# Two Mamba and mixture-of-experts layers on one core: layer 0's shared output added to X from PSUM, rows zeroed at the start, four gathers ahead, 23 tiles, layer 1's routed experts three slots later

## Chip, cores and metric

One core of a Trainium2 chip. The metric is the device time of one execution in microseconds (us), the median of several; lower is better.

## The reference

Four sublayers add to the residual stream `x` (2048 rows of 512, fp32). Twice: a selective scan over a context, gated by the normalised `x`, and then a mixture of experts of the new `x`.

```python
x = x + L0_xattn(ctx, layernorm(x))     # u = silu(conv(in_proj ctx)); state = state*exp(d*A) + d*u*B_t
                                        # y = sum_n state*C_t + D*u;  y * silu(z), z = layernorm(x)
x = x + L0_ffn(layernorm(x))
#   logits = x @ router_w; e = argmax; score = sigmoid(max)
#   out  = silu(xs @ gate_w[e]) * (xs @ up_w[e]) @ down_w[e],  xs = x * score
#   out += silu(x @ shared_gate_w) * (x @ shared_up_w) @ shared_down_w
x = x + L1_xattn(ctx, layernorm(x))     # the same form, other weights
x = x + L1_ffn(layernorm(x))            # softmax, top 2 of 8 experts of width 352,
                                        # shared expert of width 1408 times a sigmoid gate
```

Scan: 4 batches, 512 channels, 512 steps, 16 states. Experts: 8.

## The kernel before

The 2048 rows are T = 16 tiles of 128 rows, held in SBUF as `X`. All is fp32. Every engine's order is written out by hand; semaphores join the engines. Four stages stand one after the other, with the semaphores cleared between them.

**Projections** (`stage_proj`, to about 136 us) make `u` of both layers; those of layer 1, and B and C of both, go to DRAM.

**Scans** (`scan_stage`, 136 to 1434 us). 32 groups (2 layers x 4 batches x 4 channel tiles) of 16 states, 512 slots in all. A slot is `exp` on ACT into a PSUM bank (L528), `dBu` on POOL (L561), the scan on DVE (L608), the product with C on DVE (L592), and the sum over states by a matmul with the identity (L474). ACT may be at most three slots ahead of DVE's L592, POOL one ahead of L608. Four groups are a batch of 64 slots, `vb` 0 to 7; (vb, n) names a slot.

`Beside` puts layer 0's experts beside the scans, as pieces after each slot. In slots 15 to 63 of vb = 1 to 3 and 15 to 50 of vb = 4, `Shared` does one batch's four tiles: five turns r of 14 pieces m, so that down products of a tile run in the turn after its gate. It normalises into `xn` (L933), transposes, and multiplies by gate, up and down (L957). `copy_y` on ACT (L1023) takes the down product out of PSUM bank 7 into `yo`, and SP stores it in `sh_d` (L1051). `yo` is the same buffer as `sg`, so the tanh of the next tile (L1038) waits until that store has landed. `xn` is also the scratch for the tanh of the gate z (L879). At the end of vb = 4 the rows are routed; in vb = 5, `scatter` normalises and scales each tile on ACT from `X` (L1248) and POOL scatters it by expert into `xs_d` (L1256). `xs_d` was zeroed by one large DMA each (`zeros`, L424) at slot 20 of vb = 0 and 1. From slot 25 of vb = 5, `Experts` runs two pieces a slot: 24 tiles of 128 routed rows, with one buffer each for gate, up and down weights. A tile's down product again comes one turn later and its store two turns later; what is left over when the slots end runs after them.

**Layer 1's feed-forward** (`stage_ffn1`, 1434 to 2346 us). `front(b, p)` prepares batch b: add `sh_d` (L1468) and the gathered routed output of layer 0 (POOL L1416, DVE L1472) to `X`, statistics (L1475, L1478), z, silu, transposes (L1580), the new `X`, the second norm, `xTb` and the router logits (L1593). front(0) runs alone; fronts 1 to 3 run beside slots 0 to 14 of the 60 `SLOTS`, 8 sub-steps each. A slot is one 128-wide chunk of the shared expert (8 matmuls, L1612) or one tile's down product (11 matmuls, L1626). SP issues, in order: two loads of `sh_d`, the router's weights, the two halves of gate and up (2.8 MB each), the down weights (2.8 MB), and only then the next two loads of `sh_d`. Routing stands in slots 15 to 18; then POOL scatters 16 tiles to two experts each (L1453). From slot `FIRST` = 21, `Experts(1)` puts one turn of 14 pieces beside each slot: 39 tiles, of which two turns are left after the last slot.

**Combine** (`stage_combine`, 2346 to 2402 us) gathers the two rows of each token and adds them.

## Time and profile before

| | us |
|---|---|
| median of 3 runs | 2396.59 (2393.40 to 2399.49) |
| profiled execution, its own time | 2404.08 |
| span of its trace | 2402.1 |

| engine | busy us | share |
|---|---|---|
| PE (matmul) | 1959.0 | 82% |
| DVE | 1415.0 | 59% |
| POOL | 989.3 | 41% |
| ACT | 855.9 | 36% |

DMA moved 352.5 MB, 147 GB/s over the span. No engine is busy all through: the shares are means over stages with different limits. A PE record is half of an fp32 matmul here: a 128x512 product shows as two records, 0.43 us from start to start at 2.4 GHz.

### The profile page before, as it was taken

To read this page: it belongs to the slowest core of one execution; us is meant where nothing else is said; L and a number is where in the kernel's file an instruction comes from. 1 tells how busy PE (TensorE), PEld (TensorE's weight loads), DVE (VectorE), ACT (ScalarE), POOL (GpSimd) and SP (SyncE) were. 2 spreads that over 40 slices of the span, in tenths; PEclk is the share of its full clock that TensorE was granted. 3 is DMA by queue.
4 is the path that set the end of the run, shared out by engine and by line. 5 is a ranking of instruction groups with operands and counts; after the bars stand their busy time and mean duration, and the time that the engine had idled before them with its cause. 6 is when DMAs were issued, how large, how long until landed. Compare 5 with 4: busy or idle time off the path is not lost. (4 is left out here: it accounts for less than half of the span.)

```text
span 2402.1 us, 18775 instructions
## 1 busy us (share of the span) xinstructions
PE 1959.0 (82%) x5107; PEld 901.3 (38%) x5107; DVE 1415.0 (59%) x1962; ACT 855.9 (36%) x1392; POOL 989.3 (41%) x889
## 2 busy tenths in 40 slices
PE   8837678788787795599999973889599999999990
PEld 2212233233233341144444432445255555555540
DVE  6869988888887878797888844654010111111113
ACT  5545545364544444555656420110011111111110
POOL 0057766666575665887777731211400000000005
PEclk9968889899898997799999985999799999999995
DMA  5044354302203004368687645211654555455536
GB/s 185 22 194 105 140 110 107 112 5 99 89 8 153 1 14 155 138 225 339 224 305 277 215 153 189 68 50 58 242 179 152 180 180 166 160 179 180 175 123 214
DMA packets 100992, 352.50 MB, mean 147 GB/s; under 512 B 15200, under 2 KB 15200, under 8 KB 82464
## 3 DMA queue, kind: packets, MB, share of 16 engines
q1 hardware_dynamic: 93216, 326.21, 39.7%
q0 software_dynamic: 7680, 25.17, 3.1%
q8 instruction: 41, 0.67, 0.1%
q14 instruction: 55, 0.45, 0.1%
HBM read 288.29 MB, written 63.05 MB: 146 GB/s over the span
## 5 line engine op out<-in xcount | busy, mean ns | idle before, releaser
L561 POOL TENSOR_TENSOR work<-work,big 128x512 f32<-128x512 f32 x512 | 658.5, 1291 | 265.7 <-DVE bank L608 263.9
L474 PE MATMUL bank<-work,ident 128*128 128x512 f32 x928 | 536.9, 693 | 226.5 <-DVE work L592 175.9
L608 DVE TENSOR_TENSOR_SCAN bank<-bank,work 128x512 f32<-128x512 f32 x512 | 624.9, 1221 | 137.5 <-ACT bank L528 88.9
L528 ACT ACTIVATE bank<-work,An 128x512 f32<-128x512 f32 x512 | 345.9, 691 | 256.2 <-DVE work L592 253.1
L474 PEld LDWEIGHTS bank<-work,ident 128*128 128x128 f32 x928 | 179.5, 216 | 521.6 <-DVE work L592 333.7
L592 DVE TENSOR_TENSOR work<-bank,big 128x512 f32<-128x512 f32 x512 | 343.9, 672 | 9.1 <-PE bank L474 8.8
L1655 POOL DMA_INDIRECT W<-ys_d,slot x32 | 33.9, 1059 | 644.4 <-PEq L1642 634.9
L1612 PE MATMUL bank<-Y,big 128*128 128x512 f32 x528 | 263.6, 596 | 0.0
L1195 DVE SCALAR_TENSOR_TENSOR work<-work,bank 128x352 f32<-128x352 f32 (+1 forms) x63 | 36.6, 581 | 329.0 <-ACT work L1185 328.9
L957 PE MATMUL bank<-W,work 128*128 128x512 f32 x384 | 198.6, 622 | 0.0
L1173 ACT COPY work<-bank 128x512 f32<-128x512 f32 x63 | 36.9, 585 | 396.9 <-PE bank L1158 396.9
L1626 PE MATMUL bank<-big,W 128*128 128x512 f32 x352 | 169.7, 597 | 0.0
L1612 PEld LDWEIGHTS bank<-Y,big 128*128 128x128 f32 x528 | 98.8, 191 | 77.1 <-issue 48.8
L1158 PE MATMUL bank<-work 128*128 128x512 f32 (+1 forms) x234 | 115.8, 605 | 4.7 <-DMA work<-down_last 4.7
L1147 PE MATMUL bank<-work 128*128 128x352 f32 x312 | 111.5, 460 | 0.0
L1200 DVE SCALAR_TENSOR_TENSOR work<-work,bank 128x352 f32<-128x352 f32 (+1 forms) x63 | 36.6, 580 | 122.4 <-PE bank L1147 122.2
L957 PEld LDWEIGHTS bank<-W,work 128*128 128x128 f32 x384 | 75.2, 200 | 87.9 <-issue 87.9
L1137 PE MATMUL bank<-work 128*128 128x352 f32 x312 | 106.6, 465 | 1.1 <-DMA work<-gate 1.1
L1563 ACT ACTIVATE work<-bank 128x512 f32<-128x512 f32 x44 | 26.2, 596 | 220.1 <-PE bank L1612 220.1
L1158 PE MATMUL bank<-W,work 128*128 128x512 f32 x192 | 90.1, 608 | 5.6 <-DMA W<-down 5.4
L1147 PE MATMUL bank<-W,work 128*128 128x512 f32 x192 | 89.5, 604 | 0.0
L1137 PE MATMUL bank<-W,work 128*128 128x512 f32 x192 | 88.8, 593 | 0.7 <-ACT work L1166 0.7
(249 smaller groups left out, 2252.8 us busy)
## 6 DMA issues: line engine op xcount, KB each, us to landing
big<-bc_d SPq DMA_DIRECT2D x64, 1024.0 KB, 6.7
work<-gate SPq DMA_DIRECT2D x39, 704.0 KB, 4.2
work<-up SPq DMA_DIRECT2D x39, 704.0 KB, 4.1
W<-gate SPq DMA_DIRECT2D x24, 1024.0 KB, 4.9
W<-up SPq DMA_DIRECT2D x24, 1024.0 KB, 5.5
W<-down SPq DMA_DIRECT2D x24, 1024.0 KB, 5.4
work<-down SPq DMA_DIRECT2D x39, 512.0 KB, 3.8
work<-xs_d SPq DMA_DIRECT2D x63, 256.0 KB, 4.4
```

The costliest lines, as they stand in the source:

```text
L474: nc.tensor.matmul(YS[:, :], ident[:, :], hC[ring(g * NS + u[0])], start=v == 0, stop=v == len(units[g]) - 1).then_inc(sum_done, 1)
L528: nc.scalar.activation(H[i % 4][:, :], delta[g % 2], ACT.Exp, scale=An[vb // B][:, g % NJ, i:i + 1]).then_inc(dA_done, 1)
L561: nc.gpsimd.tensor_tensor(dBu[i % 2], du[g % 2], Bb[:, i, :], ALU.mult).then_inc(dBu_done, 1)
L592: nc.vector.tensor_tensor(hC[ring(s)], H[i % 4][:, :], Cb[:, i, :], ALU.mult).then_inc(hC_done, 1)
L608: nc.vector.tensor_tensor_scan(H[i % 4][:, :], H[i % 4][:, :], dBu[i % 2], 0.0, ALU.mult, ALU.add).then_inc(scan_done, 1)
L957: ins = nc.tensor.matmul(dst[:, :], at[:, c * P:(c + 1) * P], w[:, c, :], start=c == 0, stop=c == DK - 1)
L1137: ins = nc.tensor.matmul(self.G[:, 0:self.F], self.xT[q][:, c * P:(c + 1) * P], self.wg[:, c, :], start=c == 0, stop=c == DK - 1)
L1147: ins = nc.tensor.matmul(self.U[:, 0:self.F], self.xT[q][:, c * P:(c + 1) * P], self.wu[:, c, :], start=c == 0, stop=c == DK - 1)
L1158: ins = nc.tensor.matmul(self.TB[:, :], self.hT[0:fn, c * P:(c + 1) * P], self.wd[0:fn, c, :], start=c == 0, stop=c == len(self.chunks) - 1)
L1173: nc.scalar.copy(self.yo, self.TB[:, :]).then_inc(S["yo_done"], 1)
L1612: ins = nc.tensor.matmul(dst[:, :], sgu[:, c, u // DK * FS + f * P:u // DK * FS + (f + 1) * P], xTb[b][:, c, :], start=c == 0, stop=c == D ...
L1626: ins = nc.tensor.matmul(down_bank(b, r)[:, :], hT[c][:, r * P:(r + 1) * P], sdw[:, c, :], start=c == 0, stop=c == NF - 1)
```

## The change

- `Moe.tiles` is no longer made even: 23 tiles instead of 24 in layer 0.
- `copy_y`, `yo`, `sh_d`, its 16 stores and 16 loads and the 16 adds in `front` go. In `Shared.vector` DVE adds bank 7 to `X` straight away, at pieces (2,3), (3,3), (4,1) and (4,7). PE waits for `added` where it waited for `yo_done`.
- `X` then holds the shared output before the rows are scattered, so the normalised `xn` of each tile is stored in `xn_d` (SP, piece (r,6)), loaded back in vb = 5 into the scatter's row buffers, and scaled there on ACT. `norm` and the tanh into `xn` now wait for the store. 16 small copies on POOL and two small operations on DVE go.
- Both `zeros` stand in slots 0 and 1 of vb = 0, behind layer 0's weights.
- In `stage_ffn1` four gathers are under way, on four buffers; gate and up come in three pairs of loads, the first 2 chunks wide.
- `FIRST` 21 becomes 24.

```diff
-        self.tiles += (self.tiles % 2, 0)[k]
...
-                    if vb < 2 and n == 20:
-                        sp.wait_ge(hC_done, g * NS + i)
-                        zeros(vb)
+                    if g == 0 and i < 2:
+                        zeros(i)
...
             def gate(self, name, eng, b, j, i):
...
-                        self.past(eng, "xtr_done", b * NJ - NJ + (j + 1 if j else 0))
+                        used = b * NJ - NJ + (j + 1 if j else 0)
+                        self.past(eng, "xtr_done", used)
+                        self.past(eng, "xn_out", used * 16)
...
             def vector(self, dve, b, t0, n, at):
...
+                    done = {(2, 3): 0, (3, 3): 1, (NJ, 1): NJ - 2, (NJ, 7): NJ - 1}.get((r, m))
+                    if done is not None:
+                        past(dve, "d_done", t0 + done + 1)
+                        nc.vector.tensor_tensor(X[:, t0 + done, :], X[:, t0 + done, :], self.TB[:, :], ALU.add).then_inc(S["added"], 1)
...
             def norm(self, dve, b, t0, r):
...
+                self.past(dve, "xn_out", (t0 + r) * 16)
...
             def scalar(self, act, b, t0, n, at):
...
-                def copy_y(r):
-                    past(act, "d_done", t0 + r + 1)
-                    past(act, "htr_done", t0 + min(r + 2, NJ))
-                    nc.scalar.copy(self.yo, self.TB[:, :]).then_inc(S["yo_done"], 1)
-
...
-                        act.wait_ge(S["y_out"], (t0 + max(r - 1, 0)) * 16 + 1)
                         nc.scalar.activation(self.sg, self.G[:, :], ACT.Tanh, scale=0.5).then_inc(S["s_done"], 1)
...
             def sync(self, sp, b, t0, n, at):
-                for r, m in at:
-                    for tile in ([r - 2] if m == 5 and 2 <= r else []) + ([NJ - 1] if r == NJ and m == 7 else []):
-                        self.past(sp, "yo_done", t0 + tile + 1)
-                        sp.dma_start(sh_d[t0 + tile], self.yo).then_inc(self.S["y_out"], 16)
+                for tile in ([0] if n == self.START - 1 else []) + [r + 1 for r, m in at if m == 6 and r < NJ - 1]:
+                    self.past(sp, "xn_done", t0 + tile + 1)
+                    sp.dma_start(xn_d[t0 + tile], self.xn).then_inc(self.S["xn_out"], 16)
...
             def scatter(self, name, eng, t):
-                if name == "act" and 0 <= t < T:
+                if name == "sp" and 0 <= t < T:
                     if t == 0:
+                        self.past(eng, "xn_out", 16 * T)
                         eng.wait_ge(self.routed, 1)
                     if t >= 8:
                         eng.wait_ge(self.out_done[t % 8], 16)
-                    nc.scalar.activation(self.rows[t % 8], X[:, t, :], ACT.Identity, bias=nbz[:, t, 0:1],
-                                         scale=rstdx[:, t, 0:1]).then_inc(self.row_done, 1)
+                    eng.dma_start(self.rows[t % 8], xn_d[t]).then_inc(self.row_in[t % 8], 16)
+                if name == "act" and 0 <= t - 1 < T:
...
+                    nc.scalar.activation(self.rows[t % 8], self.rows[t % 8], ACT.Copy,
+                                         scale=wgt[:, 0, t:t + 1]).then_inc(self.row_done, 1)
...
-            PER_FRONT, ROUTE, FIRST = 5, 15, 21
+            PER_FRONT, ROUTE, FIRST = 5, 15, 24
+            WIDE = ((0, 2), (2, 6), (6, NF))
...
-                        at_least(pool, C["x_done"], t - 1)
+                        at_least(pool, C["x_done"], t - 3)
...
-                        if b == 0 and p < 2:
+                        if b == 0 and p < NJ:
                             gather(p)
-                        if p in (2, 3):
-                            gather(t0 + p)
-                        if b < B - 1 and p in (8, 9):
+                        if b < B - 1 and 8 <= p < 8 + NJ:
                             gather(t0 + NJ + p - 8)
...
-                            if p == r:
-                                dve.wait_ge(sh_in[t % 2], (t // 2 + 1) * 16)
-                                V.tensor_tensor(X_t, X_t, sh_b[t % 2], ALU.add).then_inc(C["sum_done"], 1)
```

On ACT, at the end of a batch of scans (the same place in vb = 1, 2 and 3). `bank<-work,An` is the exp of a slot, `COPY work<-bank` at L1023 is `copy_y`, at L1033 (L1028 in the change) the copy of the transposed h. Before:

```order
L879 ACTIVATE work<-work 128x512
L528 ACTIVATE bank<-work,An 128x512 x3
L1023 COPY work<-bank 128x512
L528 ACTIVATE bank<-work,An 128x512
L1033 COPY work<-bank 128x512
L528 ACTIVATE bank<-work,An 128x512 x3
L1023 COPY work<-bank 128x512
L528 ACTIVATE bank<-work,An 128x512 x3
```

The change:

```order
L877 ACTIVATE work<-work 128x512
L525 ACTIVATE bank<-work,An 128x512 x4
L1028 COPY work<-bank 128x512
L525 ACTIVATE bank<-work,An 128x512 x6
L868 ACTIVATE big<-X,nbz,rstdx 128x512
```

The two copies of the down product have left ACT; two and three exps that stood behind them now stand in one run with those ahead.

On SP, at the start of layer 1's feed-forward. Before:

```order
L1365 DMA work<-sh_d 128x512 x2
L1374 DMA rw<-router 128x4x9
L1378 DMA big<-sgu 128x4x1408 x2
L1379 DMA big<-sdown 128x11x512
L1365 DMA work<-sh_d 128x512 x2
```

The change:

```order
L1364 DMA rw<-router 128x4x9
L1369 DMA big<-sgu 128x4x256 x2
L1369 DMA big<-sgu 128x4x512 x2
L1369 DMA big<-sgu 128x4x640 x2
L1370 DMA big<-sdown 128x11x512
L1362 DMA xn_d<-work 128x512 x16
```

The loads on which `front` waited, two of them behind the weights, are gone.

On PE, between the router's matmuls (`bank<-work`) and the first routed tile of layer 1 (`bank<-ident,work` is its transpose). Before:

```order
L713 MATMUL bank<-work 128x128
L1612 MATMUL bank<-Y,big 128x512 x39
L1122 MATMUL bank<-ident,work 128x128 x4
L1612 MATMUL bank<-Y,big 128x512
L1137 MATMUL bank<-work 128x352 x2
```

The change:

```order
L712 MATMUL bank<-work 128x128
L1593 MATMUL bank<-Y,big 128x512 x63
L1110 MATMUL bank<-ident,work 128x128 x4
L1593 MATMUL bank<-Y,big 128x512
L1125 MATMUL bank<-work 128x352 x2
```

24 shared matmuls, three slots of 8, have come ahead of the first transpose.

## Rows read from the trace of the kernel before

**Rows 1.** Busy time by stretch: us from:to, length, each engine (xrecords), PEclk, DMA share, GB/s

```profile
285.00:950.00 665.00, 519.53 (x1250) 224.30 (x1250) 555.66 (x725) 323.73 (x490) 414.16 (x369) 0.89 0.23 76
950.00:1411.00 461.00, 412.02 (x1050) 184.97 (x1051) 385.68 (x450) 253.90 (x397) 358.12 (x286) 0.94 0.66 240
1434.00:1497.00 63.00, 15.67 (x65) 13.32 (x66) 22.59 (x45) 4.74 (x9) 10.47 (x17) 0.50 0.55 201
1497.00:1697.00 200.00, 185.48 (x558) 92.81 (x556) 109.05 (x250) 24.89 (x45) 41.77 (x65) 0.95 0.24 78
1721.00:2346.00 625.00, 619.20 (x1825) 323.25 (x1824) 84.31 (x144) 94.08 (x221) 0.00 (x0) 0.99 0.50 167
```

**Rows 2.** Waits of DVE, 285 to 950 us: for whom, us in total, times, longest

```profile
DVE bank L608 <- ACT bank L528: 40.5, 20, 5.8
...
DVE work L919 <- ACT work L1038: 21.1, 3, 7.2
```

**Rows 3.** Waits of ACT in the same stretch

```profile
ACT work L1023 <- PE bank L953: 53.4, 9, 9.1
...
ACT work L1023 <- PE bank L957: 26.3, 3, 9.0
...
ACT L1038 <- DMA sh_d<-work: 13.3, 3, 4.6
```

**Rows 4.** Timeline, end of vb = 1: start, us, engine, line, [idle before <-releaser]

```profile
440.60 0.58 ACT L1023 COPY work<-bank 128x512 f32<-128x512 f32 x1 [8.64 <-PE bank L957]
...
441.81 1.23 DVE L608 TENSOR_TENSOR_SCAN bank<-bank,work 128x512 f32<-128x512 f32 x1 [5.43 <-ACT bank L528]
```

**Rows 5.** DVE adds from PSUM (L897; ns min/median/max) and from SBUF (L1472; us, mean ns)

```profile
L897 DVE TENSOR_TENSOR X<-X,bank x16: 661/674/689, 298.4 to 800.1; 128x512 f32<-128x512 f32 x16
...
L1472 DVE TENSOR_TENSOR X<-X,work 128x512 f32<-128x512 f32 x16 | 10.9, 681 | 8.7 <-DMA work<-ys_d,slot 8.7
```

**Rows 6.** DMA issues: KB each, median us to landing

```profile
xs_d<-xds SPq DMA_DIRECT2D x1, 9984.0 KB, 52.5
```

**Rows 7.** Timeline: loads of B and C of vb = 2 asked for

```profile
255.52 0.34 SPq L419 DMA_DIRECT2D big<-bc_d  x1
```

**Rows 8.** Timeline, end of the scans and the tail behind them

```profile
1411.20 1.27 DVE L592 TENSOR_TENSOR work<-bank,big 128x512 f32<-128x512 f32 x2
...
1423.86 6.13 PE L1158 MATMUL bank<-W,work 128*128 128x512 f32 x8 [5.24 <-DMA W<-down]
```

**Rows 9.** Timeline, front(0) of layer 1's feed-forward

```profile
1434.79 1.02 POOL L1416 DMA_INDIRECT work<-ys_d,slot  x1 [24.66 <-POOLq L119]
1436.11 0.95 POOL L1416 DMA_INDIRECT work<-ys_d,slot  x1 [0.31 <-issue]
...
1464.48 0.69 DVE L1468 TENSOR_TENSOR X<-X,work 128x512 f32<-128x512 f32 x1 [19.24 <-DMA work<-sh_d]
...
1467.62 0.67 DVE L1472 TENSOR_TENSOR X<-X,work 128x512 f32<-128x512 f32 x1
```

**Rows 10.** Landing of the gathers (L1416)

```profile
DMA to landing us min/median/max: 3.3/3.7/8.3
```

**Rows 11.** Waits of PE, 1434 to 2345 us

```profile
PE bank L1580 <- DVE work L1487: 62.2, 4, 47.8
```

**Rows 12.** Timeline around slot FIRST: a run of shared matmuls, the first routed tile

```profile
1663.29 27.20 PE L1612 MATMUL bank<-Y,big 128*128 128x512 f32 x63
...
1720.72 1.11 PE L1122 MATMUL bank<-ident,work 128*128 128x128 f32 x4 [23.79 <-DMA work<-xs_d]
...
1724.64 2.69 PE L1137 MATMUL bank<-work 128*128 128x352 f32 x4 [1.10 <-DMA work<-gate]
```

**Rows 13.** Timeline: the same instruction one slot apart, and PE behind the last slot

```profile
2242.55 0.60 ACT L1563 ACTIVATE work<-bank 128x512 f32<-128x512 f32 x1 [4.41 <-PE bank L1612]
...
2257.49 0.60 ACT L1563 ACTIVATE work<-bank 128x512 f32<-128x512 f32 x1 [4.41 <-PE bank L1612]
...
2340.95 5.46 PE L1158 MATMUL bank<-work 128*128 128x512 f32 x6 [4.70 <-DMA work<-down_last]
```

More of the change, by code:

```diff
@@ L177, in program @@
         bc_d = dram("bc_d", [2 * B, 32, L])
-        sh_d = dram("sh_d", [T, P, D])
         xn_d = dram("xn_d", [T, P, D])
@@ L531, in scalar @@
                         prep(g + 1, i - y_at[g] - 3)
+                    if vb <= B:
+                        side.gate("act", act, vb, *divmod(n, NS))
                     side.step("act", act, vb, n)
@@ L820, in __init__ @@
                 self.w = w
-                made_by = {"dve": "zg_done x_done st_done mv_done xn_done h1_done h_done lg_read",
-                           "act": "z_done zt_done xT_done s_done hT_done yo_done",
+                made_by = {"dve": "zg_done x_done st_done mv_done xn_done h1_done h_done lg_read added",
+                           "act": "z_done zt_done xT_done s_done hT_done",
                            "pe": "vtr_done xtr_done g_done u_done lg_done htr_done d_done",
-                           "pool": "v_done ve_done rstd_done", "sp": "y_out"}
+                           "pool": "v_done ve_done rstd_done", "sp": "xn_out"}
                 self.made_by = {e: v.split() for e, v in made_by.items()}
@@ L853, in step @@
                 last = isinstance(b, int) and b == B
-                if not last or n < NS:
+                if name != "act":
                     self.gate(name, eng, b, *divmod(n, NS))
@@ L863, in gate @@
             def gate(self, name, eng, b, j, i):
-                first = isinstance(b, int) and b == 0
-                if first and j == 0:
+                first = b == 0
+                if first and j == 0 or b == B and j:
                     return
@@ L964, in tensor @@
                 for r, (dst, free, count) in enumerate(((self.G, "lg_read", 0), (self.U, "hT_done", 0),
-                                                        (self.TB, "yo_done", 0), (self.G, "x_done", 1))):
+                                                        (self.TB, "added", 0), (self.G, "x_done", 1))):
                     if n == self.ROUND[r]:
@@ L1001, in tensor @@
                         if r > 1:
-                            past(pe, "yo_done", t0 + r - 1)
+                            past(pe, "added", t0 + r - 1)
                         self.transpose(self.TB, self.xn, "xtr_done")
@@ L1008, in tensor @@
                             past(pe, "xT_done", t0 + min(r + 2, NJ))
-                            past(pe, "yo_done", t0 + r - 1)
+                            past(pe, "added", t0 + r - 1)
                         self.product(self.TB, self.hT, self.W0[2], m - d0, "d_done")
@@ L1027, in scalar @@
                 for r, m in at:
-                    if m == 3 and 2 <= r < NJ:
-                        copy_y(r - 2)
                     if (m == 5 if r < NJ else m == 2) and r:
@@ L1218, in __init__ @@
                 self.row_done, self.out_done = sem("t0_row_done"), [sem(f"t0_scattered{q}") for q in range(8)]
+                self.row_in = [sem(f"t0_row_in{q}") for q in range(8)]
                 self.routed, self.cleared = sem("t0_routed"), sem("t0_rows_cleared")
@@ L1234, in route @@
                         self.past(eng, "lg_read", T)
-                        self.past(eng, "rstd_done", T)
                         self.past(eng, "v_done", B * NJ)
@@ L1276, in step @@
                         eng.wait_ge(self.routed, 1)
-                        self.past(eng, "y_out", 16 * T)
+                        self.past(eng, "added", T)
+                        self.past(eng, "xn_out", 16 * T)
                     self.ex.before(name, eng)
@@ L1318, in stage_ffn1 @@
             v, zth = [wk(8 + j) for j in range(NJ)], [wk(12 + j) for j in range(NJ)]
-            sh_b, ys_b = [wk(16), wk(17)], [wk(18), wk(19)]
+            ys_b = [wk(16 + q) for q in range(4)]
             rows = [wk(14 + i) for i in range(6)]
@@ L1346, in walk @@
                             front(1 + s // PER_FRONT, s % PER_FRONT * SUB_ + u)
-                        if ROUTE <= s < FIRST:
+                        if ROUTE <= s < ROUTE + 6:
                             route(s - ROUTE, u)
@@ L1362, in _ @@
                 def _(sp):
-                    def load(t):
-                        at_least(sp, C["sum_done"], t - 1)
-                        sp.dma_start(sh_b[t % 2], sh_d[t]).then_inc(sh_in[t % 2], 16)
                     def keep(t):
@@ L1369, in keep @@
                         sp.dma_start(xn_d[t], xn[t % 2]).then_inc(xn_out[t % 2], 16)
-                    for t in range(NJ):
-                        load(t)
-                        if t == 1:
-                            sp.dma_start(rw[:, 0:DK * NL].rearrange("p (c e) -> p c e", c=DK),
-                                         w["router"].rearrange("(c p) e -> p c e", p=P)).then_inc(r_in, 16)
-                            src = w["shared_gate_up"].rearrange("(c p) f -> p c f", p=P)
-                            for c, (lo, hi) in enumerate(((0, FS), (FS, 2 * FS))):
-                                sp.dma_start(sgu[:, :, lo:hi], src[:, :, lo:hi]).then_inc(w_in[c], 16)
-                            sp.dma_start(sdw, w["shared_down"].rearrange("(c p) n -> p c n", p=P)).then_inc(w_in[2], 16)
-                    for b in range(B):
-                        for r in range(NJ):
-                            keep(b * NJ + r)
-                            if b < B - 1:
-                                load((b + 1) * NJ + r)
+                    sp.dma_start(rw[:, 0:DK * NL].rearrange("p (c e) -> p c e", c=DK),
+                                 w["router"].rearrange("(c p) e -> p c e", p=P)).then_inc(r_in, 16)
+                    src = w["shared_gate_up"].rearrange("(c p) f -> p c f", p=P)
+                    for c, (lo, hi) in enumerate(WIDE):
+                        for o in (0, FS):
+                            sp.dma_start(sgu[:, :, o + lo * P:o + hi * P], src[:, :, o + lo * P:o + hi * P]).then_inc(w_in[c], 16)
+                    sp.dma_start(sdw, w["shared_down"].rearrange("(c p) n -> p c n", p=P)).then_inc(dw_in, 16)
+                    for t in range(T):
+                        keep(t)
                     for t in range(T):
@@ L1465, in front @@
                             X_t = X[:, t, :]
[L1466 to L1468 removed]
                             if p == r + 1:
[L1470 to L1472 removed]
+                                dve.wait_ge(ga_in[t % 4], (t // 4 + 1) * 16)
+                                V.tensor_tensor(X_t, X_t, ys_b[t % 4], ALU.add).then_inc(C["x_done"], 1)
                             if p == r + 2:
@@ L1609, in shared @@
                                 at_least(pe, h_done, n - 1)
-                            if s == 0 and c == 0:
-                                pe.wait_ge(w_in[u // DK], 16)
+                            if b == 0 and u == 0 and f in [lo for lo, hi in WIDE]:
+                                pe.wait_ge(w_in[[lo for lo, hi in WIDE].index(f)], 32)
                             ins = nc.tensor.matmul(dst[:, :], sgu[:, c, u // DK * FS + f * P:u // DK * FS + (f + 1) * P], xTb[b][:, c, :],
```

30 lines of the change are left out of this document (11 added, 19 removed).

## Prediction

> **What bounds the kernel now.** I read the busy times by stretch first [rows 1], since the change touches three stages with different limits. From 285 to 950 us, where layer 0's shared expert runs beside the scans, DVE is busy 555.7 of 665 us and PE 519.5: DVE carries the loop, but 109 us of it are idle. From 950 to 1411 us PE is busy 412 of 461. From 1434 to 1497 nothing is: front(0) is a chain. From 1497 on PE is the bound (185 of 200, then 619 of 625 us), but for 24 us at 1697 in which it does nothing. So a gain is to be looked for in DVE's waits ahead of 950 us and in PE's behind 1434 us. The waits name them: DVE waits 21.1 us in three pieces for a tanh on ACT (L1038) and 40.5 us for exps [rows 2]; ACT in turn waits for the store of `sh_d`, and at `copy_y` for PE [rows 3]; PE waits 62.2 us for DVE's part of the fronts, 47.8 of them in front(0) [rows 11], and 23.8 us for the first routed rows [rows 12].
>
> **The change, step by step.** An execution that took 2404.1 us by itself is what the sum is made against; the median of three is 2396.6, 7.5 less, and I carry the difference over.
>
> *a. The store of `sh_d` goes.* It stood behind loads of B and C, so the tanh came late once in each of vb = 1, 2 and 3, and DVE stood for 21.1 us in all [rows 2]. PE stood with it. The stores of `xn_d` stand at slots 14, 19, 30 and 41, ahead of those loads (slots 51 to 63); in vb = 3 one stands behind two loads of 1 MB, with four slots in hand. I take 18 of the 21.1, since PE, which is close behind DVE, makes up some backlog there. Bounds: 0 and 21.
>
> *b. `copy_y` leaves ACT.* It waits there for PE [rows 3] with exps queued behind it. The wait of the second copy before the end of a batch (nine waits for L953) stays with the next copy, one exp later: DVE gets one more slot before it starves. I take 4 us for the four batches. The last copy is another matter: DVE starved 5.4 us for it [rows 4], and now waits itself for the same product. Bounds: 0 and 9 (some 2 per batch).
>
> *c. 16 adds come to DVE*, each 0.67 us by the add from PSUM that is already there [rows 5]. Four fall into the wait of [rows 4], which stands; 12 x 0.67 = 8 us are added. Bounds 0 (they fit into the 109 us idle) and 11. The Trainium skill, VectorE: DVE Perf Modes, section on the TRN2 errata, gives a PSUM source 62 cycles at 0.96 GHz more than an SBUF source; by it the 16 adds would be 1.0 us dearer than those removed, and the sum 2313.6. The rows have 674 ns against 681 [rows 5], so the measurement decides for no difference.
>
> *d. Zeroing first.* The larger DMA takes 52.5 us for 10 MB [rows 6]; both, 15.9 MB at that rate, 84 us. The stage begins at 136 and layer 0's weights stand ahead of them; begun by 171 us they are done by 255.5, when the next B and C are asked for [rows 7], which are needed only at 285. That cover is 30 us more than they need: 0. Without it, what runs past 285 would be lost. The 16 row loads that now precede the scatter's scaling put one DMA latency, some 4 us, into its start; ACT is up to three slots ahead, so I take 1, with bounds 0 and 4. The stores and loads of `xn_d` replace those of `sh_d`. The 16 small copies on POOL: 0, POOL is not the bound.
>
> *e. 23 tiles.* Now, behind the last product with C, which ends at 1412.5 us (1411.20 + 1.27), tile 24 still loads its down weights (PE idle 5.24), multiplies (to 1430.0), is copied and stored [rows 8], and the next stage starts at 1434. With 23, two sums and two products of tile 23 (about 3 us), the copy (0.6) and a store (2 to 3) are left: 1418.5, with the 1.4 us of the stage change 1420. That is 14 less. The last turn beside the scans has no gate and up products either, 16 records of 0.43 us on an engine that is the bound there; 2 of these 7 us. Together 16; bounds 12 and 19.
>
> *f. front(0).* DVE waits 19.24 us for `sh_d` behind 8.6 MB of weights. The gathers go through another queue and land in at most 8.3 us while those weights run [rows 10]. They are issued 1.3 us apart from 1434.8 [rows 9]; the fourth, at 1438.8, lands by 1447, and its add starts there or a little later instead of at 1467.6: 20.5, of which I take 19. From then on the chain is the same, and the weights are in long before the first product. Bounds: 2 (rival 1) and 21.
>
> *g. fronts 1 to 3.* PE waits 62.2 - 47.8 = 14.4 us in them [rows 11]. In each, four adds (0.6 apart) and waits for gathers and `sh_d` of 1 to 2 us leave DVE's chain, about 4 us: 12 us. The granted clock is 0.95 in this stretch [rows 1], the lower level of 1.2 GHz for a tenth of it, in the matmuls that follow these waits; with the waits mostly gone, 2 more. 14; bounds 7 and 19.
>
> *h. FIRST = 24.* PE stands from 1697.0 to 1720.7, when the first rows are there; the gate's weights come 4 us later, and four records of 352 columns behind them take 2.69 us, 0.67 each, where 512 columns take 0.43 at speed: the lower clock [rows 12]. Both follow from the routing, which keeps its slots. A shared slot takes 16 records at 27.20/63 = 0.43: 6.9 us. Three more reach 1697.0 + 20.6 = 1717.6, plus one product; PE then waits about 2 us for rows and 2.5 for weights. Before it lost 28.6 (27.6 to the gate's weights, less 1.3 of work, and 2.3 for a stretch at the lower clock): 24 less. Bounds 14 and 27.
>
> *i. The end of that stage.* The three displaced turns run alone. A slot with a turn takes 2257.49 - 2242.55 = 14.95 us [rows 13], so a turn is 8.1 of PE. Alone, it leaves about 5.5 us for each load of weights, of which a down load, uncovered, left PE idle for 4.70 [rows 13]. I take 2 us for the three; bounds 0 and 14.
>
> Sum: -18 -4 +8 +1 -16 -19 -14 -24 +2 = **-84**: 2320 for the profiled execution, **2312.6** for the median.
>
> **Rivals.**
> 1. *The gathers are held by the weights.* Four instead of two meet 8.6 MB. If they landed only with them, at 1464, front(0) would give 2 instead of 19: 2329.6. For it: the one gather of 8.3 us against a median of 3.7 [rows 10]. Against: it still landed, while DVE stood to 1464.5 for the `sh_d` load [rows 9]. The Trainium skill (DMA: Bandwidth & Descriptors, section on queues, rings and completion order) says that an increment lands only after every earlier write of that DMA engine, across queues, and that packets of queues alternate; taken so, a gather waits for packets begun, not for the queue. The trace agrees in that 8.3 is far from the 30 us to 1464.5. 0.09.
> 2. *PE takes DVE's place beside the scans.* PE is busy 78% there, and its backlog at the end of each batch (the 5.4 us of [rows 4]) grows when the waits of a and b go. They then give nothing and the adds cost 8: -84 + 22, 2334.6. 0.15.
> 3. *Turns alone are bound by their weights*, each stands 4.7 us: +14 instead of +2, 2324.6; or the hole at FIRST only half closes: about the same. 0.09.
> 4. *Slower: the waits go with the copies to DVE.* `copy_y` waited some 80 us on ACT [rows 3]. DVE has no slack: each us that an add waits stops the scan. The rest of the sum, with c's 8 us left in, is -84; so at 84/16 = 5.3 us of waiting per add the change breaks even, and with 6 it ends at 2408.6. Against it: DVE is one to three slots (2.5 us each) behind ACT when it comes to the add, and two thirds of the wait are for L953, for which the add does not wait. 0.03.
>
> That the tiles or `FIRST` do not change what they say is excluded by the order of instructions.
>
> **How the numbers follow.** The forecast has 0.62, rivals 1 to 4 0.09, 0.15, 0.09 and 0.03, and 0.02 is left for no change in effect. The low end takes the better bounds of a, b, f, g and h together (-3 -5 -2 -5 -3) and of e (-3, -1 for c): 2290; the high end takes rival 2 with a part of 1 or 3: 2345. A measurement of this kernel can tell about 0.3% (7 us) from no change. Faster: 0.95; same 0.02; slower 0.03.
>
> **What would show it.** Right: no wait of L1038 for a store and no DVE idle of 7 us ahead of 950; 16 new adds with short waits, but for four of some 4 us; the scan stage ending near 1403 instead of 1434; the four gathers landing in under 9 us, and the first shared matmul (now 1496.4) some 29 us behind the last add as now; PE waits in fronts 1 to 3 of about 1 us; under 6 us of PE idle at slot 24; the last three turns 8 to 9 us apart. Wrong: adds that wait 3 us and more throughout, PE idle of over 10 us at slot 24, a last turn of 12 us, or waits of ACT for `xn_d`.

## The result, and the profile after

| | before | after |
|---|---|---|
| median | 2396.85 us (4 runs) | 2303.82 us (4 runs, 2298.09 to 2305.58) |
| ratio to before | | 0.9609, 95% interval 0.9588 to 0.9629 |
| profiled execution, its own time | 2404.08 | 2298.09 |
| span of its trace | 2402.1 | 2296.4 |

The change takes 93 us off the median; 84 were forecast (2312.6, range 2290 to 2345). The two profiled executions are 106 us apart, because that of before lies 7 above its median and that of after 6 below. So what the two traces add up to is 106, and 13 of it is spread between executions of the same kernel, not the change. Where that matters below, medians decide.

The sum over the states of a group of scans ends at L597 before and at L596 after, so its start dates each group in both traces. With some other instructions that both kernels have, it shows where the 106 us appear (gain so far, and gain in the step):

| instant | before | after | so far | step |
|---|---|---|---|---|
| group 3 summed (end of vb = 0) | 282.4 | 282.6 | -0.2 | -0.2 |
| group 7 | 445.3 | 438.0 | 7.3 | 7.5 |
| group 11 | 609.1 | 591.5 | 17.5 | 10.2 |
| group 15 | 773.1 | 745.1 | 28.0 | 10.4 |
| group 19 (end of vb = 4) | 952.2 | 916.0 | 36.2 | 8.3 |
| group 20 | 1000.5 | 967.0 | 33.5 | -2.8 |
| group 31 (end of the scans) | 1416.5 | 1381.2 | 35.3 | 1.9 |
| first gather of the next stage | 1434.8 | 1387.7 | 47.1 | 11.8 |
| last add of front(0) | 1467.6 | 1398.4 | 69.2 | 22.1 |
| routing begins (first CAST) | 1655.2 | 1570.2 | 85.0 | 15.8 |
| last down product | 2341.0 | 2237.3 | 103.7 | 18.7 |
| end of the span | 2402.1 | 2296.4 | 105.7 | 2.0 |

**Beside the scans.** Busy times of the same work in both traces: first before, from 285 us to the end of vb = 4, then after (each engine, with its number of records, then PEclk, DMA share, GB/s).

```profile
285.00:953.00 668.00, 519.54 (x1251) 224.31 (x1251) 558.66 (x729) 326.73 (x494) 416.06 (x371) 0.89 0.24 77
```

```profile
285.00:917.00 632.00, 502.76 (x1251) 213.60 (x1252) 569.25 (x743) 317.34 (x472) 413.87 (x355) 0.92 0.17 66
```

The third engine is DVE. It works 10.6 us more (16 adds) in 36 us less: its idle time falls from 109.3 to 62.8. What it waits for in that stretch after the change (for whom, us, times, longest):

```profile
DVE bank L607 <- POOL work L560: 23.1, 16, 1.6
DVE X L916 <- PE bank L959: 15.4, 5, 4.1
DVE work L921 <- ACT work L1032: 6.1, 3, 2.0
DVE Y L596 <- PE bank L471: 4.7, 5, 2.3
...
DVE bank L607 <- ACT bank L525: 2.9, 10, 0.3
```

Against [rows 2] the waits for the tanh fell from 21.1 to 6.1 and those for exps from 40.5 to 2.9. New are 15.4 us at the adds (L916), nearly all of it in four waits of 4 us at the ends of the batches. The end of vb = 1 on the timeline after, where [rows 4] had DVE idle 5.43 us for an exp behind a copy on ACT:

```profile
421.52 0.59 ACT L1028 COPY work<-bank 128x512 f32<-128x512 f32 x1 [3.50 <-PE bank L955]
...
433.92 0.69 DVE L916 TENSOR_TENSOR X<-X,bank 128x512 f32<-128x512 f32 x1 [4.06 <-PE bank L959]
```

**The end of the scans and front(0).** Timeline after, to be held against [rows 8, 9]:

```profile
1377.93 1.27 DVE L591 TENSOR_TENSOR work<-bank,big 128x512 f32<-128x512 f32 x2
...
1382.88 0.59 ACT L1161 COPY work<-bank 128x512 f32<-128x512 f32 x1 [8.70 <-PE bank L1146]
...
1387.68 1.02 POOL L1403 DMA_INDIRECT work<-ys_d,slot  x1 [9.46 <-POOLq L118]
...
1393.83 0.69 DVE L1453 TENSOR_TENSOR X<-X,work 128x512 f32<-128x512 f32 x1 [11.92 <-DMA work<-ys_d,slot]
...
1398.44 0.68 DVE L1453 TENSOR_TENSOR X<-X,work 128x512 f32<-128x512 f32 x1
...
1426.35 16.07 PE L1593 MATMUL bank<-work,big 128*128 128x512 f32 x30
```

From the last product with C (ends 1379.2) to the first gather are 8.5 us where there were 22.3. The four adds then follow each other with a wait only before the first and one of 0.53 us before the second. The gathers landed in (source line L1403, us min/median/max):

```profile
DMA to landing us min/median/max: 3.4/4.9/6.8
```

**From there on.** Waits of PE from 1387 to 2300 us after, against [rows 11], and the timeline at slot FIRST and at the last product, against [rows 12, 13]:

```profile
PE bank L1561 <- DVE work L1468: 30.9, 4, 25.8
PE bank L1146 <- DMA work<-down_last: 4.5, 1, 4.5
PE bank L1110 <- DMA work<-xs_d: 3.2, 1, 3.2
...
PE bank L1125 <- DMA work<-gate: 2.3, 1, 2.3
```

```profile
1635.76 0.66 PE L1110 MATMUL bank<-ident,work 128*128 128x128 f32 x4 [3.21 <-DMA work<-xs_d]
...
1639.59 2.68 PE L1125 MATMUL bank<-work 128*128 128x352 f32 x4 [2.26 <-DMA work<-gate]
...
2237.26 4.51 PE L1146 MATMUL bank<-work 128*128 128x512 f32 x6 [4.48 <-DMA work<-down_last]
```

PE's waits for the fronts are 30.9 where they were 62.2; of these the one in front(0) is 25.8 where it was 47.8, those in fronts 1 to 3 are 5.1 where they were 14.4. For the shared weights, which now come in three pairs of loads, PE waits in neither trace; no run changes that split alone. The wait for the first routed rows is 3.2 where it was 23.8.

### The profile page after: what moved, and what is told of

The parts are those of the page before. It is cut to its first block and busy times, and to the rows that moved or that the text cites. A ratio compares the mean times of both kernels' runs of the same rounds, so it can differ in the third digit from the quotient of the medians.

```text
span 2296.4 us, 18644 instructions
## 1 busy us (share of the span) xinstructions
PE 1920.6 (84%) x5075; PEld 877.6 (38%) x5075; DVE 1415.4 (62%) x1958; ACT 846.8 (37%) x1372; POOL 984.7 (43%) x873
## 5 line engine op out<-in xcount | busy, mean ns | idle before, releaser
L471 PE MATMUL bank<-work,ident 128*128 128x512 f32 x928 | 528.5, 683 | 213.2 <-DVE work L591 162.6
L471 PEld LDWEIGHTS bank<-work,ident 128*128 128x128 f32 x928 | 173.3, 209 | 512.6 <-DVE work L591 335.1
L1593 PE MATMUL bank<-Y,big 128*128 128x512 f32 x528 | 258.7, 594 | 0.0
L959 PE MATMUL bank<-W,work 128*128 128x512 f32 x384 | 190.8, 600 | 0.0
L1498 DVE SCALAR_TENSOR_TENSOR W<-work,bank 128x512 f32<-128x512 f32 x44 | 30.2, 686 | 94.9 <-PE bank L1593 94.7
L1135 PE MATMUL bank<-W,work 128*128 128x512 f32 x184 | 88.2, 618 | 0.5 <-DMA W<-up 0.5
L1607 PEld LDWEIGHTS bank<-big,W 128*128 128x128 f32 x352 | 65.2, 190 | 58.7 <-issue 46.0
```

The costliest lines, as they stand in the source:

```text
L471: nc.tensor.matmul(YS[:, :], ident[:, :], hC[ring(g * NS + u[0])], start=v == 0, stop=v == len(units[g]) - 1).then_inc(sum_done, 1)
L959: ins = nc.tensor.matmul(dst[:, :], at[:, c * P:(c + 1) * P], w[:, c, :], start=c == 0, stop=c == DK - 1)
L1135: ins = nc.tensor.matmul(self.U[:, 0:self.F], self.xT[q][:, c * P:(c + 1) * P], self.wu[:, c, :], start=c == 0, stop=c == DK - 1)
L1593: ins = nc.tensor.matmul(dst[:, :], sgu[:, c, u // DK * FS + f * P:u // DK * FS + (f + 1) * P], xTb[b][:, c, :], start=c == 0, stop=c == D ...
L1607: ins = nc.tensor.matmul(down_bank(b, r)[:, :], hT[c][:, r * P:(r + 1) * P], sdw[:, c, :], start=c == 0, stop=c == NF - 1)
```

## The experiments

Each kernel is the changed one with one thing altered (or, at the end, a second one on top), timed beside the kernel before on the same chip. The kernel before had medians of 2395.4 to 2398.9 us in these series and 2396.9 beside the change, so a gap between two kernels of different series carries some 2 us of that. The ratios, which take it out, have 95% intervals by which a gap is known to some 6 to 8 us. Gaps of that size or less (copy_dh, copy_d, hold_weights, late_down, late_down25) therefore need their traces beside them.

How far can a single trace be trusted? That depends on the stage. Five kernels (the change, first21, gathers2, tiles24, hold_weights) have the same program up to group 19, and end it at 915.96 to 922.54 us, 6.6 apart. Behind the scans the spread is far smaller: from the first gather to the last add of front(0) the eleven kernels with four gathers and the loads in the change's order take 10.7 to 11.1 us, and from the routing to the start of the last down product the ten with FIRST = 24 and the old place for the last down weights take 665.9 to 667.9.

The largest open point was that the scans gained some 35 us up to their end, where the prediction's terms a to d and the 2 us of e give 15. I first rebuilt on the changed kernel, piece by piece, what had gone.

**copy_dh: ACT's two waits again.**

```diff
+                    done = {(2, 3): 0, (3, 3): 1, (NJ, 1): NJ - 2, (NJ, 7): NJ - 1}.get((r, m))
+                    if done is not None:
+                        past(act, "d_done", t0 + done + 1)
+                        past(act, "htr_done", t0 + min(done + 2, NJ))
+                        nc.scalar.copy(self.spare[:, :], ident[:, :])
```

> The changed kernel, but ACT again stops at the four places per tile batch where copy_y stood, for the same two things (the down product, and the transposed h of the tile two further on), and then copies a small SBUF tile (128x128). DVE's adds stay. Theory 1 (term b was sized too small: the exps held behind the waiting copies cost DVE some 20 us over the four batches, not 4): ACT waits over 60 us at the 16 places, DVE waits for exps rise from 5.9 us towards 30 between 285 and 920 us, and the time is 2303.8 + 15 to 22 = 2319 to 2326. Theory 2 (term b was right at 4 us; the 36 us that the scans gained came from the store, from PE or from the clock): 2304 to 2310.

Measured: 2310.5 us (4 runs, 2307.8 to 2312.3), 0.9634 of before (0.9617 to 0.9651): 6.7 more than the change (by the ratios 6.0, known to about 6), between the theories. Group 19 ends at 928.6 in its trace, 12.7 later than in that of the change, 6.1 to 12.7 later than in the five above. Waits from 285 to 925 us, ACT's (the new instruction is L1030), then one of DVE's:

```profile
ACT spare L1030 <- PE bank L956: 47.5, 9, 8.7
ACT spare L1030 <- PE bank L960: 34.7, 4, 10.4
```

```profile
DVE bank L607 <- ACT bank L525: 14.2, 20, 1.6
```

ACT waits 82 us, and DVE's waits for exps come back to 14.2, half of what was expected.

**copy_d: only the wait for the down product.** The same edit without the `htr_done` line.

> The same, but ACT waits at those 16 places for the down product alone, not for the transposed h. Theory 1a (what cost was the wait for the transposed h, which copy_y needed because its target was the buffer of h): no more than 5 us over the changed kernel, 2304 to 2309, and ACT waits some 25 us there. Theory 1b (any wait for PE on ACT costs): 2315 to 2325, as with both waits.

Measured: 2310.2 us (2307.9 to 2316.3), 0.9644 (0.9625 to 0.9664); group 19 at 927.2. ACT now waits for the down product alone, 71.9 us where it waited 82.2 for both:

```profile
ACT spare L1029 <- PE bank L960: 71.9, 13, 10.4
```

This is theory 1b, with a smaller price: dropping the wait for the transposed h changes nothing that can be seen (2310.2 against 2310.5). That ACT waits for PE at all costs 6 to 7 us by the medians, 11 to 13 by these traces, of which up to 6.6 can be the spread of the change's own.

**full_a: and the store of `sh_d`.** On top of copy_dh:

```diff
+                        act.wait_ge(S["y_out"], (t0 + max(r - 1, 0)) * 16 + 1)
                         nc.scalar.activation(self.sg, self.G[:, :], ACT.Tanh, scale=0.5).then_inc(S["s_done"], 1)
...
+                        self.past(sp, "yo_done", t0 + tile + 1)
+                        sp.dma_start(sh_d[t0 + tile], self.sg).then_inc(self.S["y_out"], 16)
```

> copy_dh and, on top of it, the store that the changed kernel removed: SP stores the buffer sg (the h of the tile) to DRAM behind each of those 16 places, and the next tanh into sg waits until it has landed, as before. Term a alone, beside the waits of copy_dh. The end of the scans of vb = 4 came 36.2 us earlier with the change, and copy_dh gives 12.7 of them back. If a is 18 us as predicted: DVE waits for the tanh rise from 6.1 to about 21 us, and the time is 2310.5 + 15 = 2325 (2320 to 2330). If the store was in the shadow of the other waits: under 2315.

Measured: 2326.3 us (2325.4 to 2330.8), 0.9704 (0.9688 to 0.9720): 15.8 more than copy_dh; group 19 at 945.5, 16.9 later. The waits of before are there again, DVE's for the tanh and ACT's for the store (285 to 950 us):

```profile
DVE work L923 <- ACT work L1040: 20.9, 3, 7.0
```

```profile
ACT L1040 <- DMA sh_d<-work: 14.8, 3, 5.0
```

Term a is confirmed in place and in size (by the ratios 16.8, known to about 6).

**thin_add: the adds almost without work.** `X[:, t0 + done, 0:8]` and `TB[:, 0:8]` in place of 512 columns, so that 504 of 512 columns of layer 0's shared output are left out of `X`.

> The changed kernel, but the 16 adds of DVE from bank 7 take 8 columns instead of 512 (so 504 of 512 columns of layer 0's shared output are left out of X); they stand where they stood, with their waits. It measures the work of term c, not its waits. If DVE is the bound (c = 8 us as predicted, 12 x 0.6): 2303.8 - 7 to 10 = 2294 to 2297. If the adds fitted into time that DVE waits anyway: 2301 to 2304, with DVE's waits for POOL or ACT longer by as much.

Measured: 2291.4 us (2290.2 to 2294.8), 0.9563 (0.9547 to 0.9580): 12.4 less than the change, 8.6 less by group 31 of the traces (1372.5 against 1381.2). A thin add still takes 0.152 us (median of L916 in its trace) against 0.676, so what was taken out is 16 x 0.524 = 8.4 us. The traces give it back in full, the medians a little more (by the ratios 11.0, known to about 6): DVE is the bound, and hardly any of an add is hidden. A whole add then costs its 0.676 us, 16 of them 10.8.

**full_b: the scans of before, as far as they can be rebuilt.** full_a with thin adds, and ahead of the last copy of a batch:

```diff
+                        if done == NJ - 1:
+                            act.wait_ge(S["y_out"], (t0 + NJ - 1) * 16 + 1)
```

> full_a with the one wait it left out (the last copy of a batch waits on ACT for the store before it), and with DVE's adds cut to 8 of 512 columns, as in thin_add (504 columns of layer 0's shared output are left out of X). It is the kernel before as far as the scans go, but for where the sum is taken. If terms a, b and c are all of it: from vb = 1 to the end of vb = 4 (group 19) the scans take as long as before, 952 us (full_a 945.5, before 952.2, thin adds alone 5.5 less than the change), and the time is 2326.3 - 9 + 7 = 2324. If the missing wait gives nothing, group 19 ends at 938 to 941 us and the time is 2312 to 2320: then 12 us of the gain are still without a cause.

Measured: 2326.6 us (2323.5 to 2329.3), 0.9704 (0.9679 to 0.9729). By the median this is the time expected if a, b and c are all there is; by its trace it is the other case: group 19 ends at 939.1, 13 ahead of before. The median is 22.7 above that of the change, and this kernel has no adds to speak of, as before had none. What is left to before, 2396.9 - 2326.6 = 70.3, is close to what the other parts give (below: e 15.1, h and i 16.4, the fronts 38, the row loads -2.8: 66.7). So the medians close to within 4 us, which is less than they are known to, and two single traces don't. The reason is the spread told above: group 19 ends at 915.96 in the change, 916.00 (first21), 916.09 (gathers2), 921.65 (tiles24) and 922.54 (hold_weights). PE's granted clock explains it in part at most: from 750 to 905 us it is 0.92 in the trace of the change, 0.87 in that of tiles24, but 0.90 in those of first21 and gathers2, which end as early as the change. The profiled execution of before is 7.2 above its median and that of full_b 3.0 below its own, which would be 10 of the 13. Whether the rest is spread too is not settled, for the rebuild is not the kernel before. Its copy takes 128 columns of SBUF and not 512 of bank 7. And its DVE still stands at the thin adds for 16.6 us, where before had no adds, and waits 20.6 us for exps where before waited 40.5 (285 to 940 and 285 to 950 us).

**late_add: the last add of a batch later.**

```diff
-(NJ, 7): NJ - 1}
+(NJ, 7): NJ - 1 if isinstance(b, int) and b == B else None}
...
+                if n == 2 and t0:
+                    past(dve, "d_done", t0)
+                    nc.vector.tensor_tensor(X[:, t0 - 1, :], X[:, t0 - 1, :], self.TB[:, :], ALU.add).then_inc(S["added"], 1)
```

> The changed kernel, but the last add of each of the batches beside vb = 1, 2 and 3 stands in slot 2 of the next batch of scans instead of three slots before the end. DVE now waits some 4 us there, four times (15.4 us in five waits). Theory 1 (that wait is pure loss, since nobody needs the sum so early): 3 x 2.5 to 4 us less, 2292 to 2297. Theory 2 (PE's backlog is what is waited for; DVE then waits as long for PE at the sum over states): no change, 2301 to 2306, with waits of the add gone and waits of DVE for the sum (L471) of 3 to 4 us in their place.

Measured: 2293.3 us (2292.0 to 2296.9), 0.9570 (0.9554 to 0.9586): 10.5 less than the change. This is the time of theory 1. DVE's waits from 285 to 925 us:

```profile
DVE Y L596 <- PE bank L471: 11.4, 8, 2.5
...
DVE X L919 <- PE bank L962: 3.1, 2, 1.8
```

12.3 of the 15.4 us at the adds have gone, and of those 6.7 show up at the sum over states, so theory 2 has a part in it too: 5.6 are left, and group 19 ends 5.0 earlier than in the change. The median gives 10.5 (by the ratios 9.3, known to about 6). The sign is sure, the size lies between 5 and 10.

**first21: FIRST back.** `PER_FRONT, ROUTE, FIRST = 5, 15, 21`.

> The changed kernel with FIRST = 21 again: term h undone alone. By the trace of the change, what FIRST = 24 gave is 18.6 us (from the first gate product of the routed tiles to the last down product 597.7 us against 616.3), so 2322.4; by the prediction's own terms h and i it is 24 - 2 = 22, so 2325.8. The rival, that the hole would have closed partly by itself with the shorter fronts: under 2315. PE should stand about 24 us at the first transpose of routed rows.

Measured: 2320.2 us (2314.9 to 2326.4), 0.9682 (0.9656 to 0.9708): 16.4 more by the median. In the traces it takes 686.1 us from the first CAST of the routing to the last down product where the change takes 667.1: 19.1, or 18.2 to 20.2 against the ten traces. PE waits again as in [rows 12]:

```profile
PE bank L1110 <- DMA work<-xs_d: 23.9, 1, 23.9
```

**tiles24: the 24th tile back.** `self.tiles += (self.tiles % 2, 0)[k]`.

> The changed kernel with 24 tiles in layer 0 again: term e undone alone. By its sum (14 behind the scans, 2 beside them) 2303.8 + 16 = 2320 (2316 to 2323), with PE idle some 5 us for the last down weights behind the scans. If the tail had been hidden by something else in the next stage: under 2312.

Measured: 2318.9 us (2314.6 to 2320.8), 0.9662 (0.9636 to 0.9688): 15.1 more. From the last product with C to the first gather its trace has 22.6 us, the change 8.5. PE's wait behind the scans is back:

```profile
PE bank L1147 <- DMA W<-down: 5.3, 1, 5.3
```

**gathers2: two gathers ahead.** `at_least(pool, C["x_done"], t - 1)`, and the gathers at p < 2, 2, 3, 8 and 9 again.

> The changed kernel with two gathers ahead instead of four, in the places where the kernel before had them. It splits terms f and g (22 and about 15 us by the trace of the change): how much is the loads of sh_d gone, how much the gathers. If the loads of sh_d were what was waited for: each pair of gathers costs one landing of 4 to 6 us in front(0) and 1 to 2 us in fronts 1 to 3: 2303.8 + 7 to 12 = 2311 to 2316. If the order of the gathers mattered as much as the loads: over 2320. If neither: 2304 to 2307.

Measured: 2318.4 us (2312.5 to 2322.5), 0.9672 (0.9646 to 0.9697): 14.6 more than the change. That is above the 2311 to 2316 expected if only the loads of `sh_d` mattered, and short of the 2320 at which the gathers would matter as much. PE's waits for the fronts:

```profile
PE bank L1563 <- DVE work L1470: 40.8, 4, 30.2
```

From the end of the scans to the first shared product it takes 50.5 us (45.2 with four), from there to the routing 154.0 (143.9). Of those 10.1 us, 5.5 are waits (10.6 in fronts 1 to 3 instead of 5.1), and the granted clock in that stretch is 0.94 instead of 0.98. From the first gather to the last add it takes 15.2 us instead of 10.8. So the gathers are 4 to 5 of the 22 us of front(0), the loads of `sh_d` 17 to 18; in fronts 1 to 3 the gathers are 10 of 15.8.

**hold_weights: the gathers first.**

```diff
+                    for q in range(4):
+                        sp.wait_ge(ga_in[q], 16)
                     for c, (lo, hi) in enumerate(WIDE):
```

> The changed kernel, but SP issues layer 1's shared weights only when the first four gathers have landed. It tests what is left of rival 1 (gathers held by the weights): with the change the gathers took 4.9 us (median) against 3.7, and DVE began the first add 6.1 us after its gather was issued. If the weights hold them: the first add comes 2 us sooner, and the weights, which then end some 7 us later, are still in time for the first product: 2301 to 2303. If they don't hold them: no change, or worse where the first product then waits for weights: 2304 to 2308.

Measured: 2310.5 us (2306.0 to 2314.6), 0.9638 (0.9616 to 0.9659): 6.7 more. The weights do hold the gathers: the sixteen now land in 3.6 us in the median instead of 4.9, DVE's wait for the first is 9.21 instead of 11.92, and from the first gather to the last add it takes 7.6 us instead of 10.8. But DVE then stands for something else, the buffer of the third tile's normed x, since the store of the first hasn't landed (waits of DVE from 1390 to 1560 us; then SP's queue):

```profile
DVE work L1485 <- DMA xn_d<-work: 11.7, 1, 11.7
```

```profile
1404.93 5.12 SPq L1372 DMA_DIRECT2D big<-sdown  x1
1414.97 17.56 SPq L1362 DMA_DIRECT2D xn_d<-work  x4
```

The first store was issued at 1415.0, 15 us after the first of 8.6 MB of weights, and DVE went on at 1430.1, 15 us later. In the changed kernel the same store was issued 26 us after the first of the weights (1413.2), and DVE went on 5.5 us later, after a wait of 2.3. The first shared product then starts 45.1 us after the first gather instead of 38.7 (39.5 to 39.9 in ten other traces), which is the loss. I had not followed that store behind the later weights.

**late_down: the last down weights to another buffer.** On top of late_add: for the last tile `down` is loaded to `sdw[:, 0:3, :]`, free since the shared expert's last product, with a semaphore of its own.

```diff
+                    if self.last and isinstance(t, int) and t == N:
+                        sp.wait_ge(self.last[1], T)
+                        self.load(sp, t - 1, self.last[0], "down", "last_in")
```

> late_add, and the down weights of the very last routed tile of layer 1 go to the buffer of the shared expert's down weights, which is free by then, so that their load need not wait for the tile before. PE stands 4.5 us for them now. If that wait is what sets the end: 2293.3 - 4 = 2289 (2287 to 2291), and PE has no wait for down_last. If the h of that tile comes as late as the weights: 2292 to 2294, with a wait of PE for the copy of h in its place.

Measured: 2289.5 us (2287.4 to 2292.7), 0.9553 (0.9536 to 0.9570): 3.8 less than late_add, as expected; the medians alone could not tell so little. In the traces it takes 663.9 us from the routing to the last product, against 666.4 in late_add and 665.9 to 667.9 in the ten. Between the last two steps of PE 0.78 us are left, for ACT:

```profile
2229.12 2.84 PE L1158 MATMUL bank<-big,work 128*128 128x512 f32 x6 [0.78 <-ACT work L1181]
```

**late_down25: and FIRST = 25.**

> late_down with FIRST = 25. At 24 PE still stands 3.3 us for the first routed rows and 1.6 us for the gate's weights; a fourth displaced turn costs 8 to 9 us instead of 8.1 beside a slot. If the rest of the hole is worth more than the extra turn alone: 2289.5 - 3 to 4 = 2286. If the turn alone eats it: 2288 to 2291.

Measured: 2281.7 us (5 runs, 2275.9 to 2289.2), 0.9518 (0.9491 to 0.9546), the fastest kernel here: 7.8 less than late_down, where 3 to 4 were expected. The medians are of two series and their ratios know that gap to about 8 only, but from the first CAST to the last product it takes 656.8 us against 663.9, 7.1 less in a stretch that repeats within 2. The window from 1575 to 1640 us, late_down and then late_down25:

```profile
1575.00:1640.00 65.00, 60.75 (x137) 27.10 (x136) 20.52 (x61) 5.36 (x9) 31.04 (x32) 0.92 0.60 200
```

```profile
1575.00:1640.00 65.00, 65.00 (x158) 29.31 (x157) 22.20 (x65) 5.96 (x10) 30.98 (x32) 1.00 0.59 200
```

The holes were 4.3 us, and with them gone PE also keeps the clock it lost behind them: a granted clock of 0.92 over 65 us is 5.2 us short of full clock. In the same 65 us PE does 158 records instead of 137; 19 of the 21 more have 512 columns, so that is 21 x 0.43 = 9 us of work more. I had priced the hole and left out the clock behind it. 9 less the 7.1 leaves 2 for the fourth turn that runs alone, an estimate by difference.

## Why the prediction was right, by its own steps

*What bounds the kernel* held: DVE beside the scans (thin_add), a chain in front(0), PE after.

*a. The store, 18.* Right: 15.8 by full_a against copy_dh, 16.9 in the traces; DVE's waits fell by 15.0.

*b. `copy_y` off ACT, 4, bounds 0 and 9.* Undone alone it costs 6.7 us by the medians, inside the bounds, and 12.7 in the traces, beyond them. But the profiled execution of the change lies 5.7 below its median and that of copy_dh 1.4 above, 7 us together, so the term is at most sized somewhat too small. "DVE gets one more slot before it starves" counted one exp per batch; DVE's waits for exps fell from 40.5 to 2.9 us, and came back to 14.2 in copy_dh and to 20.6 in full_b, so more exps than those were held. That the wait at the end of a batch stands, now at the add, was right (4.06 against 5.43). That wait is also a price of the change that can be avoided: late_add moves one instruction and takes out 10.5 us by the medians, 5 in the traces.

*c. 16 adds, 8.* Too small, a little: thin_add takes 8.4 us of the adds' 10.8 out and gains 12.4, or 8.6 in the traces. I left four adds out because they fell into a wait; by either number few hid. An add from PSUM takes 0.676 us (L916, median) and one from SBUF 0.678 (L1453, mean), so [rows 5] were right. By the 62 cycles at 0.96 GHz that the Trainium skill gives (VectorE: DVE Perf Modes, section on the TRN2 errata) the first would be longer by an estimate of 65 ns; this trace does not agree.

*d. Zeroing and the row loads, 1.* The zeroes cost nothing: vb = 0 ends at 282.6 against 282.4. The row loads cost 2.8, in group 20, where ACT waited 9.3 us for the first; that is inside the bound of 4.

*e. 23 tiles, 16.* Right: 15.1 by tiles24; its trace has 14.1 of them between the last product with C and the first gather, where 14 were forecast.

*f and g. The fronts, 19 and 14.* Right: 22.1 and 15.8 in the traces. The trace of the change is the shortest of eleven in fronts 1 to 3 (171.8 us from the last add of front(0) to the routing, against 172.3 to 173.7), so 14 would fit as well. What was not foreseen is the split, above: in fronts 1 to 3 most of it is the two more gathers.

*h and i. FIRST, 24 less 2.* Too large: 16.4 by first21, 18.7 to 19.1 in the traces. The step that failed here is "2.3 for a stretch at the lower clock": the change still has a hole of 5.5 us, and its first four gate records still take 2.68 us as before. Three slots of 6.9 are 20.6, less the 2 for the turns alone: 18.6. These turns came 9.4, 8.6 and 9.3 us apart, where 8 to 9 were expected.

*The rivals.* Gathers held by the weights: in small part. They land in 6.8 us at most, and hold_weights shows that the weights cost 3.1 us up to the last add of front(0). The Trainium skill (DMA: Bandwidth & Descriptors, section on queues, rings and completion order) has each DMA engine go round its queues packet by packet. That gathers landed within 6.8 us while 8.6 MB of another queue were on the way agrees with it. PE in DVE's place: did not come, for then thin_add would have gained nothing. Waits moved to DVE: 15.4 us, 1 per add, where 5.3 were needed to turn the result round. Turns bound by their weights: not but for the last.

*Of the signs to look for*, the end of the scan stage was furthest off: the first gather is at 1387.7, not near 1403, but up to 13 of these 15 us are the distance of the two profiled executions from their medians. The waits of PE in fronts 1 to 3 are 5.1 in all, the longest 3.5, not 1 each.

*The sum.* By medians of the undone parts: a 15.8, b 6.7, e 15.1, h and i 16.4, the fronts 38 (traces), the row loads -2.8 (trace), and the adds -12.4: together 76.8 of 93. full_b, which undoes a, b and c at once, has 22.7 where these three give 10.1 one by one; with it the sum is 22.7 + 15.1 + 16.4 + 38 - 2.8 = 89.4. So what the single terms miss lies in the scans. The medians would have it that the waits of ACT and the adds of DVE bear on each other: with ACT's waits in place, thin adds gained nothing (full_b against full_a, though that pair also differs by one wait), without them 12.4. But the difference between this 12.4 and that nothing is known only to some 10 us, and the traces don't bear it out: group 19 ends 6.4 us earlier in full_b than in full_a, and 5.6 earlier in thin_add than in the change. How the rest divides, and whether the parts bear on each other at all, isn't settled.

*What was luck.* Set against the numbers undone one by one, the forecast of 84 was too large by 15 in a, c, d, e, h and i (2.2, 4.4, 1.8, 0.9, 5.6), too small by 8 in b, f and g (2.7, 5), and lacked the 16 us by which the parts fall short of the whole. That it came within 9 of the 93 is owed in part to these offsetting each other. The mechanisms of a, e, f and g stand by themselves.

## What to carry to other kernels

A wait for another engine, placed on an engine that feeds the critical one, costs what is queued behind it, not what it does; price it by the feed and not by the copy. Here ACT waited 82 us in copy_dh, for copies of a 128x128 tile, and the kernel lost 6.7. When such a wait moves to the critical engine itself, look for a later place at once: the adds three slots ahead of the end of a batch stood 15.4 us in all, and with three of them two slots into the next batch 3.1, though 6.7 came back at the sum over states. And a hole on PE has two prices, its length and the lower clock behind it, so that the last 4 us of a hole were worth about twice their length here.

## What the runs showed of the hardware that I had not expected

Closing holes of 4.3 us on PE gave 7 to 8 us, since the granted clock over the 65 us around it went from 0.92 to 1.00. Five traces of the same program up to the end of vb = 4 had it end at 916.0 to 922.5 us: in the scans a single trace of this kernel settles no term under 6 us. Behind the routing ten traces agree within 2.0 us of some 667, so there a trace settles more than the medians do. And a store of 256 KB issued 15 us after the first of 8.6 MB of loads on the same queue let DVE go on 15 us later, and stopped it for 11.7; issued 26 us after them, it took 5.5 and stopped it for 2.3.
